# A two-layer mixer kernel: L1's recurrent state over 128 partitions, the up weights' split in the first step, L1's weights loaded behind the decay rows

## The reference

```python
xn = layernorm(x)
x = x + L0_attn(xn) + L0_ffn(xn)     # Mamba2 (state 16, 8 heads of 64) with an MLP behind it; soft tree of depth 8
xn = layernorm(x)
x = x + L1_attn(xn) + L1_ffn(xn)     # Mamba2 (state 64, 4 heads of 128); 8 experts, each takes its 1024 best tokens
```

```python
h = rmsnorm(x, norm2_w)
h = silu(h @ mlp_w1 + mlp_b1) @ mlp_w2 + mlp_b2        # 256 -> 1024 -> 256

def step(state, inp):                                  # L1: state is (batch, 4 heads, 128, 64)
    dA = jnp.exp(dt_t * A)
    state = state * dA + dt_t * x_t * B_t
    y_t = einsum('bhpn,bn->bhp', state, C_t) + D * x_t
```

## Time and profile before

| | |
|---|---|
| median of 3 runs | 1555.44 us (1549.87 to 1558.59) |
| the profiled execution's own time | 1551.76 us |
| its span | 1549.8 us |
| mean granted clock of TensorE | 0.965 |
| PE busy | 1445.4 us, 93% of the span |
| DVE busy | 1071.8 us, 69% |
| ACT busy | 726.1 us, 47% |
| POOL busy | 533.6 us, 34% |
| chain that ended last | PE 64%, issue 15%, DVE 9%, POOL 7% |

### The profile page before, as it was taken

How to read it: one execution, slowest core, us unless ns; L and a number is a source line. 1 busy time by engine, 2 the same in 40 slices (tenths; PEclk the granted TensorE clock), 3 DMA queues, 4 the chain that set the end, 5 groups by cost and what they waited for, 6 DMA issues and landing times.

```text
span 1549.8 us, 22663 instructions
## 1 busy us (share of the span) xinstructions
PE 1445.4 (93%) x7315; PEld 1057.7 (68%) x7315; DVE 1071.8 (69%) x2549; ACT 726.1 (47%) x1468; POOL 533.6 (34%) x631
## 2 busy tenths in 40 slices
PE   6889999999999999988689998999899999999996
PEld 4556767686767768677345555455578988888895
DVE  6969685867768686831798888889875465645542
ACT  4252433426262533422456555666465554655552
POOL 1334234242524243331123232332235333544343
PEclk9999999999999999998799999999999999999998
DMA  8020301103030202110501211112034333523322
GB/s 260 14 60 23 97 28 54 69 1 122 0 109 14 96 27 65 46 41 1 180 18 65 68 38 66 49 57 65 28 97 85 93 61 93 111 70 73 84 52 27
DMA packets 71846, 100.90 MB, mean 65 GB/s; under 512 B 13000, under 2 KB 58192, under 8 KB 71760
## 3 DMA queue, kind: packets, MB, share of 16 engines
q1 hardware_dynamic: 59472, 82.77, 16.3%
q0 software_dynamic: 12288, 17.05, 6.5%
HBM read 74.30 MB, written 25.49 MB: 64 GB/s over the span
## 4 chain that ended last, share of the span: by engine, by line
PE 64%; issue 15%; DVE 9%; POOL 7%; SPq 1%; ACT 1%; DMA 1%; DVEq 0%; POOLq 0%; ACTq 0%
PE bank L2131 59%; DVE u L1503 3%; POOL yb L952 2%; POOL Xs L944 2%; SPq L591 1%; POOL ry L960 1%; PE bank L2240 1%; PE bank L2208 1%; PE bank L2506 1%; DVE am L1946 1%; POOL out L1010 1%; PE bank L2337 1%; DVE xo L1664 1%; POOL xg L983 1%; PE bank L2266 0%
## 5 line engine op out<-in xcount | busy, mean ns | idle before, releaser
L2090 DVE TENSOR_TENSOR aml<-m0big,amh 128x512 fp32r<-128x512 f32 x128 | 88.2, 690 | 175.8 <-ACT amh L1352 167.0
L1010 POOL DMA_INDIRECT out<-EW,IDX x64 | 104.2, 1629 | 220.7 <-DVE EW L2085 206.1
L1347 ACT ACTIVATE m0big<-bank,eb 128x512 f32<-128x512 f32 x128 | 87.9, 687 | 162.1 <-PE bank L2131 139.8
L2131 PE MATMUL bank<-w2h,amh 128*128 128x256 f32 x512 | 148.0, 289 | 0.0
L2131 PE MATMUL bank<-w2h,aml 128*128 128x256 f32 x512 | 144.8, 283 | 0.0
L2131 PE MATMUL bank<-w2l,amh 128*128 128x256 f32 x512 | 144.7, 283 | 0.0
L1127 ACT ACTIVATE am<-bank,b 128x512 f32<-128x512 f32 x64 | 44.0, 687 | 157.4 <-PE bank L2131 156.8
L2131 PE MATMUL bank<-EW,am 128*128 128x256 f32 x512 | 115.8, 379 | 0.0
L2131 PEld LDWEIGHTS bank<-EW,am 128*128 128x128 f32 x512 | 97.3, 190 | 13.4 <-ACT am L1127 0.3
L2131 PEld LDWEIGHTS bank<-w2h,amh 128*128 128x128 f32 x512 | 97.6, 191 | 8.3 <-issue 5.8
L2131 PE MATMUL bank<-xTh,w1h 128*128 128x512 f32 x256 | 102.1, 399 | 0.6 <-DVE xTl L2011 0.6
(11 more groups left out here) (342 smaller groups left out, 3693.1 us busy)
## 6 DMA issues: line engine op xcount, KB each, us to landing
EW<-in_e_w SPq DMA_DIRECT2D x16, 1024.0 KB, 5.7
dA0b<-dA_d SPq DMA_DIRECT2D x16, 512.0 KB, 3.9
E<-dA_d SPq DMA_DIRECT2D x16, 512.0 KB, 5.4
m0big<-dA_d SPq DMA_DIRECT2D x16, 512.0 KB, 4.8
xin<-in_L_attn_x SPq DMA_DIRECT2D x8, 512.0 KB
xp<-in_L_attn_x SPq DMA_DIRECT2D x8, 512.0 KB, 3.7
rows_d<-xo SPq DMA_DIRECT2D x8, 512.0 KB, 3.0
x_d<-xb SPq DMA_DIRECT2D x8, 512.0 KB
```

The costliest lines, as they stand in the source:

```text
L1010: g.indirect_dma_start(out=out_rows, out_offset=bass.IndirectOffsetOnAxis(ap=IDX[:, 4 * u + c:4 * u + c + 1], axis=0), in_=ye[:, q, c, :], ...
L1347: a.activation(am2[:, j % 2, :], bank[j % 2][:, :], ACT.Gelu, bias=eb1[:, u // 2, j:j + 1]).then_inc(gelu_sig.sem, 1)
L2090: v.tensor_tensor(aml[:, j % 4, :], am2[:, j % 2, :], amh[:, j % 4, :], ALU.subtract).then_inc(am_low.sem, 1)
L2131: return t.matmul(out_, lhsT, rhs, start=first, stop=last)
```

## The change

Three parts.

First, loads. The list of 15 is split: w1, n2w and b1 stay at their place under a semaphore of their own (`w_up`); the other 12 go into `load_rest`, which SP issues behind `decays_of(0)` and before `later_decays_of(0)`. The wait of DVE's `rest_of_mixer` for `w_rest` is added beside ACT's.

Second, the up weights. The four products that make the high parts go from DVE to ACT (`up_weights_high`, Copy with a scale for each partition), in ACT's first L0 step behind chunk 1's copies. The four low parts stay on DVE and move into its first L0 step, two in `first_residual` behind h and two behind xn, before `dt_raw`.

Third, L1's state. It is kept in 128 partitions by 256 columns: heads 0 and 1 in partitions 0 to 63, heads 2 and 3 in 64 to 127. DVE's update takes two operations of 128 partitions by 128 columns, with decays from a small table `EXS` that two copies fill at L1's start. On PE "inter" becomes two products of 256 columns, one for each half of the partitions; the second stands behind "state" now, and only it tells ACT that "inter" is filled. "state" becomes two products of 256 columns that write partitions 0 to 63 and 64 to 127. So that C is at hand in both halves, `silu1` runs its second Silu over all 128 partitions, behind its own first one.

```diff
-        S = sb("S", [64, DI])
+        SS = sb("S", [P, DI])
+        S, S1 = SS[0:64, :], SS[:, 0:2 * P]
...
+        EXS = dA0b[:, 7 * P:7 * P + 2 * TILES]
...
-            square_load(w1, "w1", w_rest)
...
-            load(v["gn"][:, :], d["m1_gn"], w_rest)
+            square_load(w1, "w1", w_up)
+            load(n2w[:, :], d["n2w"], w_up)
+            load(b1[:, :], d["b1"], w_up)
+
+            def load_rest():
+                square_load(w2, "w2", w_rest)
+                square_load(wr[:, :, 0:NE], "wr", w_rest)
...
+                square_load(v["out"][:, :, :], "m1_wo", w_rest)
+                load(v["gn"][:, :], d["m1_gn"], w_rest)
...
             decays_of(0)
+            load_rest()
             later_decays_of(0)
...
+            def up_weights_high():
+                act.wait_ge(w_up, 16 * W_UP)
+                for k in range(KD):
+                    for half in range(2):
+                        a.activation(W1H[k][half], w1[:, k, half * HID // 2:(half + 1) * HID // 2], ACT.Copy,
+                                     scale=n2w[:, k:k + 1]).then_inc(up_high, 1)
+
...
                             chunk(L, s, f, c + 1)
+                        if isinstance(f, int) and f == 0 and c == 0:
+                            up_weights_high()
                         if c:
...
-                    a.activation(ub[0:64, 4, :], ub[0:64, 4, :], ACT.Silu).then_inc(s1.xc.sem, 1)
+                    s1.xc.wait_ge(act, i, 1)
+                    a.activation(ub[:, 4, :], ub[:, 4, :], ACT.Silu).then_inc(s1.xc.sem, 1)
...
-            def rest_of_weights():
+            def up_weights_low(k):
...
-                dve.wait_ge(w_rest, 16 * W_REST)
-                for k in range(KD):
-                    for a in range(2):
-                        v.tensor_scalar(W1H[k][a], w1[:, k, a * HID // 2:(a + 1) * HID // 2], n2w[:, k:k + 1], None,
-                                        ALU.mult, ALU.bypass).then_inc(prepped, 1)
-                        count += 1
-                dve.wait_ge(prepped, count)
-                for k in range(KD):
-                    for a in range(2):
-                        v.scalar_tensor_tensor(out=W1L[k][a], in0=w1[:, k, a * HID // 2:(a + 1) * HID // 2],
-                                               scalar=n2w[:, k:k + 1], in1=W1H[k][a], op0=ALU.mult,
-                                               op1=ALU.subtract).then_inc(prepped, 1)
-                        count += 1
-                assert count == PREPPED_UP, count
+                dve.wait_ge(up_high, 2 * KD)
+                for half in range(2):
+                    v.scalar_tensor_tensor(out=W1L[k][half], in0=w1[:, k, half * HID // 2:(half + 1) * HID // 2],
+                                           scalar=n2w[:, k:k + 1], in1=W1H[k][half], op0=ALU.mult,
+                                           op1=ALU.subtract).then_inc(prepped, 1)
+                    count += 1
...
+                dve.wait_ge(w_rest, 16 * W_REST)
...
-                if isinstance(b, int) and b == 0:
-                    rest_of_weights()
...
                         residual(0)
+                    if isinstance(f, int) and f == 0:
+                        up_weights_low(0)
                     if f is not None:
...
                         residual(c)
+                if isinstance(f, int) and f == 0:
+                    up_weights_low(1)
+                    assert count == PREPPED_UP, count
                 if n is not None:
...
-                    v.memset(S[:, :], 0.0).then_inc(s1.S.sem, 1)
+                    v.memset(S1, 0.0).then_inc(s1.S.sem, 1)
...
-                for k in range(NH1):
+                for k in range(NH1 // 2):
...
-                    ins = v.scalar_tensor_tensor(out=S[:, sl], in0=S[:, sl],
-                                                 scalar=EX[0:64, 2, NH1 * n + k:NH1 * n + k + 1],
-                                                 in1=p[0:64, sl], op0=ALU.mult, op1=ALU.add)
+                    ins = v.scalar_tensor_tensor(out=S1[:, sl], in0=S1[:, sl],
+                                                 scalar=EXS[:, 2 * n + k:2 * n + k + 1],
+                                                 in1=p[:, sl], op0=ALU.mult, op1=ALU.add)
...
+            for half in range(2):
+                rows = slice(64 * half, 64 * (half + 1))
+                op(v.tensor_copy(EXS[rows, :].rearrange("p (t k) -> p t k", k=2),
+                                 EX[rows, 2, :].rearrange("p (t h) -> p t h", h=NH1)[:, :, 2 * half:2 * half + 2]))
...
-                cb, n = CB[i % 2], CH * i + c
+                ub, cb, n = UB[i % 2], CB[i % 2], CH * i + c
...
-                filled1(mm(p[:, :], cb[:, cols(c)], S[:, :]), "inter")
+                mm(p[:, 0:2 * P], cb[0:64, cols(c)], S1[0:64, :]).then_inc(s1.half.sem, 1)
...
-                p = open1("state", n)
-                filled1(mm(p[0:64, :], Bs[:, c % 2, :], Xs[:, c % 2, :]), "state")
+                r = open1("state", n)
+                mm(r[0:64, 0:2 * P], Bs[:, c % 2, :], Xs[:, c % 2, 0:2 * P])
+                filled1(mm(r[64:P, 0:2 * P], Bs[:, c % 2, :], Xs[:, c % 2, 2 * P:4 * P]), "state")
+                s1.half.wait_ge(pe, i, c + 1)
+                filled1(mm(p[:, 2 * P:4 * P], ub[64:P, 4, cols(c)], S1[64:P, :]), "inter")
```

More of the change, by code:

```diff
@@ L51 @@
 AXX = mybir.AxisListType.X
-W_FUSE, W_DT, W_X, W_LATE, W_REST = 4, 5, 4, 4, 15
-PREPPED_DT, PREPPED_X, PREPPED_FUSED, PREPPED_FIRST, PREPPED_UP, PREPPED = 8, 10, 15, 21, 29, 34
+W_FUSE, W_DT, W_X, W_LATE, W_UP, W_REST = 4, 5, 4, 4, 3, 12
+PREPPED_DT, PREPPED_X, PREPPED_FUSED, PREPPED_FIRST, PREPPED_UP, PREPPED = 8, 10, 15, 21, 25, 30
 EARLY_UPS, LATE_UPS = (0, 1, 2, 3), ((4,), (5,), (6,), (7,))
@@ L354, in program @@
         w_fuse, w_dt, w_x, w_late = (sem(n) for n in ("w_fuse_loaded", "w_dt_loaded", "w_x_loaded", "w_late_loaded"))
-        w_rest = sem("w_rest")
+        w_up, w_rest = sem("w_up_loaded"), sem("w_rest")
+        up_high = sem("w1_high_ready")
         consts = sem("consts")
@@ L434, in program @@
             s0.yT, s0.x2, s0.S))
+        s1.half = sig(n + "inter_half", CH)
         s1.E, s1.M, s1.rv = (sig(n + name, CH) for name in ("decays", "mask_ready", "y_var"))
@@ L630, in _ @@
             load(w["gn"][:, :], d["m0_gn"], w_late)
-            square_load(w1, "w1", w_rest)
-            square_load(w2, "w2", w_rest)
-            load(n2w[:, :], d["n2w"], w_rest)
-            square_load(wr[:, :, 0:NE], "wr", w_rest)
-            load(b1[:, :], d["b1"], w_rest)
-            square_load(wr[:, :, NE:NR], "m1_wdt", w_rest)
-            square_load(v["bc"][:, :, :], "m1_wbc", w_rest)
-            square_load(v["x"][:, :, :], "m1_wx", w_rest)
-            square_load(v["z"][:, :, :], "m1_wz", w_rest)
-            load(v["conv"][:, :, :], d["m1_conv"], w_rest)
-            load(v["dtb"][:, :], rows("m1_dtb", LAYERS[1].heads), w_rest)
-            load(v["A"][:, :], rows("m1_alog", LAYERS[1].heads), w_rest)
-            load(v["D"][:, :], rows("m1_D", LAYERS[1].heads), w_rest)
-            square_load(v["out"][:, :, :], "m1_wo", w_rest)
-            load(v["gn"][:, :], d["m1_gn"], w_rest)
+            square_load(w1, "w1", w_up)
[4 more added lines that the diff above has]
+                square_load(wr[:, :, 0:NE], "wr", w_rest)
+                square_load(wr[:, :, NE:NR], "m1_wdt", w_rest)
+                square_load(v["bc"][:, :, :], "m1_wbc", w_rest)
+                square_load(v["x"][:, :, :], "m1_wx", w_rest)
+                square_load(v["z"][:, :, :], "m1_wz", w_rest)
+                load(v["conv"][:, :, :], d["m1_conv"], w_rest)
+                load(v["dtb"][:, :], rows("m1_dtb", LAYERS[1].heads), w_rest)
+                load(v["A"][:, :], rows("m1_alog", LAYERS[1].heads), w_rest)
+                load(v["D"][:, :], rows("m1_D", LAYERS[1].heads), w_rest)
+                square_load(v["out"][:, :, :], "m1_wo", w_rest)
+                load(v["gn"][:, :], d["m1_gn"], w_rest)
             def store_back(b):
@@ L1792, in op @@
                 dve1.see(dve)
-            v.memset(S[:, :], 0.0).then_inc(prepped, 1)
+            v.memset(SS[:, :], 0.0).then_inc(prepped, 1)
             v.memset(xbuf[:, :, 0:4], 0.0).then_inc(prepped, 1)
```

## The result

| | before | changed |
|---|---|---|
| median | 1553.14 us (18 runs, 1549.87 to 1558.79) | 1561.3 us (18 runs, 1556.98 to 1566.92) |
| ratio to before | | 1.0052, 95% interval 1.004 to 1.0065: 8.1 us slower |
| profiled execution | 1551.76 us | 1560.85 us |
| L1's tiles begin at | 770.66 us | 764.46 us |
| from there to the first yT copy's end | 21.8 us | 27.0 us |

In the profiled executions the first steps gained 6.2 us; L1 gave back 5.2 at its head and 9.7 in its tiles.

A forecast was written before the change was run, and what follows sets the result against it. PE was taken to bound L0's steps, but neither PE nor DVE nearly bound L1. Terms -3.4 - 5.7 + 3.2 = -5.9 against the profiled 1551.8 gave 1545.9, predicted median 1549.5; forecast's own range 1544 to 1555, overall 1538 to 1562.

The forecast's parts named there:

- L1's typical step: Four such steps in L1: PE's wait before x's transposes and the half-clock stretch behind it go; -1.3 each, -5.2 together.
- Part 1, -3.4: First step: decay rows' load issued earlier, 2.7 us gained on DVE plus 0.7 from faster matmuls; ends 0 and -3.5.
- Part 2, -5.7: Up products start 4.4 us earlier without DVE's weight work, and 1.3 from no half-clock stretch; ends -4.4 and -6.0.
- It arrives whole: The 5.7 us gained at the up products reaches the total, because the L0 steps behind are bound by PE.
- The covers: Two pairs of differences on DVE, 1.4 us each, fit before waits of 1.92 and 2.33; without cover each costs 1.4.
- Part 3, +3.2: L1's total: losses from later projections and longer PE loops, less gains from the shorter state update and vanished waits; +3.2 us.
- the first cycle: L1's first cycle, with the longest wait for the state update, gains 2.1 us.
- the step with the wait of 1.98: L1's step with the shortest wait before x's transposes loses 0.9 us, PE being late by more than the wait.
- the one without a wait: L1's step with no wait for the update loses the full 0.5 + 0.5 + 1.7 + 1.7 = 4.4 us.
- first rival: Slow stretches stay in L1, as PE's idle time moves rather than vanishes; L1 costs 9.9, time 1556; chance 0.20.
- second rival: More slow stretches than before in L1, each costing 2.8 us; one in each of six steps gives 1573; chance 0.13.
- third rival: The two "state" products run side by side on PE in L1, 0.5 back per loop, -6.5, time 1543; chance 0.17.

The follow-up runs named there:

- part 2 alone: The kernel before with only the up weights' change, all loads at their old place and L1 as before: 1548.21 us, ratio 0.998.
- filled changed kernel: The changed kernel plus unused identity products on PE ahead of waits in L1's loops of c = 2 and 3: 1557.91 us, ratio 1.0035.
- part 3 alone: The kernel before with only the change to L1's state, the first steps as before: 1568.46 us, ratio 1.0093.
- part 1 with its first wait filled: The kernel before with only the loads' change, plus nine identity products ahead of PE's wait at 42.4 in the first step: 1555.66 and 1556.11 us.

## Why the prediction was wrong

- The step that failed most is the one in L1's typical step: I let the half-clock stretch behind the wait before x's transposes go with that wait ("the stretch is gone"), worth 2.8 in each of four steps. The wait went and the stretch stayed, and the four steps came to +4.9 in sum where I had -5.2. The other terms are below.
- Part 1, -3.4: the load (at 26.98) and the scan (at 32.94) came as said. The 2.7 for DVE was 1.5: x times dt began at 37.24, behind a wait of 1.78 for B's rows of PE that my sum did not have, and the next scan took 0.8 more than before. The half clock at 47.56 was to give back 0.7; in four profiles with part 1 it lasted 17 us instead of 6.8 at that place, which the ends that I gave for this part, 0 and -3.5, had no room for. Measured over all executions part 1 is worth about nothing: -1.1 and +0.5 in two comparisons.
- Part 2, -5.7: L1 began 4.65 earlier with part 2 alone; by the ratio the gain is 3.1 (1.2 to 4.8). The 4.4 of DVE's work came off, but the first up product came only 2.6 earlier, because PE itself was later there (the wait of 2.47 for `dtv` and the stretch behind it, above). "It arrives whole" failed; the stretch behind the first up product went, and 2.05 more came behind it, where I had 1.3. The covers held on DVE in the changed kernel: the first pair took 2.20 for 1.4 and filled its wait, the second left 1.01 of its own.
- Part 3, +3.2, measured +14.4 (10.4 to 18.6). Its prices were near: 1.3 measured for a loop of c = 2 or 3 where I said 1.7, 0.23 for c = 0 and 1 where I said 0.53. The second half costs 0.63, and "state" gives back 0.39, which I had only as a rival. The update is 0.60, as forecast.
- The sum of the typical step, -1.3. The wait before x's transposes fell from 2.9 to 0.2 at 905 us, as I said, and the stretch of 6.8 us behind it stayed. From one c = 1 loop to the next step's, the typical steps measured +1.2, +0.9, +0.7 and +2.1. In the filled changed kernel two of these steps (tiles 9 to 17) have no half clock at all, and they measure -1.3 and -1.1: with the stretch gone the sum is right. That is luck in part, since the stretch was worth about 2 there (2.15 and 1.77, against the changed kernel without filler) and not 2.8, and the loops cost less than I had said. I had taken from the kernel before that nothing there shows a drop behind waits of about 1 us. That reading was wrong: the stretch at 83 us, in L0, followed waits of 0.74, 0.69 and 1.22.
- The rest of L1's sum, changed kernel against before: the first cycle -0.5 for -2.1, the step with the wait of 1.98 +2.2 for +0.9, the one without a wait +3.1 for +4.4, the last four tiles +1.5 for +4.5 (it lies inside the +2.1 above), the head +5.2 for +0.7 (+1.4 in part 3 alone).
- So the first rival, 1556, had the right mechanism in L1, the stretches staying, and my sum for it was short by the same sort of error: first steps gained 5.9 and not 9.1, and the loops lost 9.7 to 13.5. The second rival added slow stretches: in part 3 alone 54.6 us of half clock against 41.0, in the changed kernel 47.8. The filled changed kernel puts the clock's share of the 9.7 us lost in the tiles at 4.5; the late projection, which was in my sum, is the other half.
- The Trainium skill, "TensorE: Matmul & The Clock Gate", section on a second HAM failure mode, says that short idle times of PE between groups of matmuls can make the clock swing between its levels; I weighed it against the rows and set it aside. The trace agrees in part: waits of 0.17, 0.30 and 0.85 stood in front of the stretch at 909, while the loop at 1110 to 1116, with 0.85 twice, ran at full clock.
- The third rival's mechanism came true beside the forecast's failure. The Trainium skill, "TensorE: Matmul & The Clock Gate", Part 3 on packing small matmuls, says that matmuls in distinct column groups run concurrently. The trace agrees: 0.58 for the pair against 0.98 into the same partitions, a factor of 1.7.
- I also did not ask the question that mattered: whether the moved half needed to be behind "state" at all. The wait in front of "state" was in my rows (0.42, to become 0.95) and was the cover.

## What to carry to other kernels

When work is moved behind a wait, look first whether that wait was its cover: half of a product placed ahead of it was free, placed behind it cost 0.6 us in two of four loops and 1.4 in the other two, where it also made the next engine late. A shorter operation on one engine is worth only what its reader waits for; write down the other waits of the same loop and what is one step behind each. And when a sum counts on the clock coming back once a wait is gone, price the case in which it doesn't, and look for stretches at half clock in every stage of the trace, not only in the one that changes.

## What was not expected of the hardware

- Two f32 products of 256 columns with 64 weight columns each, into partitions 0 to 63 and 64 to 127 of one bank, took 0.58 together; into the same partitions 0.98.
- Stretches at half clock came with no wait over 0.85 us in front of them (at 909, 1005 and 1101 us), and could be cut by 30 us or more in L1 by multiplying identities in PE's waits, with no other work removed.
- A stretch of 17 us can come in one execution of a kernel and not in another: part 1 with its first wait filled had none before 130 us in one profile (L1's tiles from 767.54) and one at 69 us in the other (774.14).
